# Merged additions, leaky units and stores in the three tails of a graph network

## What is computed

```python
def _sage_conv(x, src, dst, Wl, bl, Wr):
    agg = jax.ops.segment_max(x[src], dst, num_segments=x.shape[0])
    agg = jnp.where(jnp.isfinite(agg), agg, 0.0)
    return agg @ Wl + bl + x @ Wr

h = jnp.maximum(_layernorm(x, axis=-1), 0.0)
h = leaky_relu(_sage_conv(h, src, dst, Wl1, bl1, Wr1), 0.01)   # 128 -> 256
h = leaky_relu(_sage_conv(h, src, dst, Wl2, bl2, Wr2), 0.01)   # 256 -> 256
h = leaky_relu(_sage_conv(h, src, dst, Wl3, bl3, Wr3), 0.01)   # 256 -> 128
return x + h
```

## Time and profile before

| what | us |
|---|---|
| median of 3 runs | 6159.85 |
| lowest and highest of them | 6159.41, 6161.66 |
| the profiled execution, its own time | 6166.19 |
| its span | 6164.4 |
| tail of layer 0, first end-row gather to the next layer's first gather | 2004.00 to 2076.39 |
| tail of layer 1, the same | 4048.95 to 4121.35 |
| tail of layer 2, first end-row gather to the end of the span | 6094.30 to 6164.4 |

### The profile page before, as it was taken

The page is one execution under the profiler, slowest core; times in us unless marked ns, Lnnn a source line. Parts: engine busy times, 40 slices in busy tenths (PEclk is TensorE's granted clock), DMA queues, the critical chain, the costliest instruction groups (busy, mean ns, idle before and its releaser), DMA issues. The chain is left out here.

```text
span 6164.4 us, 24445 instructions
## 1 busy us (share of the span) xinstructions
PE 691.8 (11%) x2214; PEld 397.6 (6%) x2214; DVE 2907.7 (47%) x3633; ACT 227.4 (4%) x662; POOL 4617.2 (75%) x4877
## 2 busy tenths in 40 slices
PE   0111111111100770000000000056000000000003
PEld 0000000000000430000000000044000000000002
DVE  4333333333333555555555555565555555555556
ACT  1000000000000110000000000011000000000001
POOL 6777777777777777777777777767777777777776
PEclk7555555555555655555555555565555555555556
DMA  4333333333333576666666666667666666666665
GB/s 138 106 109 105 107 107 106 107 107 105 108 104 106 181 233 210 210 210 210 207 210 210 208 210 209 210 211 244 210 210 207 210 210 209 210 208 210 210 207 176
DMA packets 434293, 1088.81 MB, mean 177 GB/s; under 512 B 100293, under 2 KB 152778, under 8 KB 434266
## 3 DMA queue, kind: packets, MB, share of 16 engines
q0 software_dynamic: 206976, 530.17, 31.4%
q1 hardware_dynamic: 204506, 539.02, 23.2%
q10 hardware_dynamic: 22784, 19.34, 1.0%
HBM read 555.06 MB, written 533.07 MB: 177 GB/s over the span
## 5 line engine op out<-in xcount | busy, mean ns | idle before, releaser
L394 POOL DMA_INDIRECT ring<-features,stage x4692 | 4449.2, 948 | 1454.6 <-issue 1401.5
L715 DVE TENSOR_TENSOR ring<-banks,ring 128x1024 f32<-128x1024 f32 (+1 forms) x1173 | 1226.9, 1046 | 3057.5 <-DMA ring<-features,stage 3040.3
L687 DVE TENSOR_TENSOR banks<-ring,banks 128x1024 f32<-128x1024 f32 (+1 forms) x1173 | 1231.9, 1050 | 37.5
L940 PE MATMUL banks<-ident,ring 128*128 128x128 f32 x20 | 5.0, 428 | 3772.8 <-DVEq L727 3772.8
L914 PE MATMUL banks<-dst_low,own 128*128 128x394 bf16 x200 | 98.9, 495 | 1465.8 <-DVE own L663 1465.8
L940 PEld LDWEIGHTS banks<-ident,ring 128*128 128x128 f32 x20 | 3.9, 222 | 3774.2 <-DVEq L727 3548.7
L898 PE MATMUL banks<-wr,h_turned 128*128 128x256 f32 (+1 forms) x490 | 202.7, 556 | 96.2 <-ACT h_turned L1032 96.2
L1076 ACT ACTIVATE agg<-zeros 128x512 f32<-128x512 f32 x75 | 47.3, 630 | 3955.9 <-PE banks L971 3955.9
L421 POOL DMA_INDIRECT ring<-running_max_log,end_row x147 | 142.5, 970 | 67.4 <-issue 43.9
L668 DVE COPY stage<-edges 128x8 int32 (+1 forms) x588 | 143.1, 243 | 84.8 <-DVE banks L687 25.8
L900 PE MATMUL banks<-b,ones 1*128 1x256 f32 (+1 forms) x294 | 140.3, 573 | 0.0
(11 more groups left out here) (110 smaller groups left out, 571.1 us busy)
## 6 DMA issues: line engine op xcount, KB each, us to landing
running_max_log<-ring SPq DMA_DIRECT2D x782, 512.0 KB, 3.3
running_max_log<-ring SPq DMA_DIRECT2D x391, 256.0 KB, 2.2
ring<-features,stage POOLq DMA_INDIRECT x4692, 2.8
h_in<-features ACTq DMA_DIRECT2D x98, 128.0 KB, 2.8
features<-h_out SPq DMA_DIRECT2D x48, 256.0 KB, 2.3
h_in<-features ACTq DMA_DIRECT2D x49, 64.0 KB, 1.8
out<-h_out SPq DMA_DIRECT2D x24, 128.0 KB, 2.3
ring<-running_max_log,end_row POOLq DMA_INDIRECT x147, 2.9
```

The costliest lines, as they stand in the source:

```text
L394: pool.indirect_dma_start(ring[:, c * w:(c + 1) * w], None, tables[l], bass.IndirectOffsetOnAxis(ap=stage[:, b, u:u + 1].bitcast(U32), axi ...
L687: dve.tensor_tensor(sum_ps[:, 0:CHAINS * w].rearrange("p (h f) -> p h f", h=CHAINS), group(g - 1).rearrange("p (h f) -> p h f", h=CHAINS), ...
L715: dve.tensor_tensor(group(g), sum_ps[:, 0:CHAINS * w], group(g), ALU.max).then_inc(turn, 1)
```

## The change

From now on a tail has units: `UNITS` joins pairs 0 and 1, 2 and 3, up to 18 and 19 into ten units of two pairs, and pairs 20 to 24 stay alone (`SINGLES = 5`), 15 units in all. `add_own`, `leaky`, `residual` and the store work on a unit: an addition or leaky unit of a double unit is 2 x 2n wide, 1024, 1024 and 512 elements in the three layers. A double unit's addition stands on DVE behind the `guard` of the pair after the unit, its leaky unit one step later. The projections use four neighbouring PSUM banks (1 to 4) in turn, so that a double unit lies in two neighbouring banks; `z_sum` has two buffers of twice the size, `h_out` three of twice the size. `add_own` waits in addition until the unit two before it is done, and PE waits for the unit that held its bank. `mask`, `guard` and `turn_pair` stay pair by pair.

```diff
-STORES = 5
+STORES = 3
+SINGLES = 5
...
+    UNITS = [(q, q + 1) for q in range(0, PAIRS - SINGLES, 2)] + [(q,) for q in range(PAIRS - SINGLES, PAIRS)]
+    UNIT_OF = [u for u, pairs in enumerate(UNITS) for _ in pairs]
...
-        z_sum = [sb(f"z_sum{b}", [P, 2 * F_MAX]) for b in range(3)]
-        h_out = [sb(f"h_out{k}", [P, 2 * F_MAX]) for k in range(STORES)]
+        z_sum = [sb(f"z_sum{b}", [P, 4 * F_MAX]) for b in range(2)]
+        h_out = [sb(f"h_out{k}", [P, 4 * F_MAX]) for k in range(STORES)]
...
-        mm_ps = [banks[:, 1, :], banks[:, 2, :], banks[:, 3, :]]
+        mm_ps = banks[:, 1:5, :]
...
+                def of_unit(u):
+
+                    first, pairs, wide = UNITS[u][0], len(UNITS[u]), PAIR_TILES[UNITS[u][0]] * n
+
+                    def rows(tile, at):
+                        return tile[:, at:at + pairs * wide].rearrange("p (k f) -> p k f", k=pairs)
+
+                    b = first % 4
+                    return (mm_ps[:, b:b + pairs, 0:wide], rows(z_sum[u % 2], 0), rows(h_out[u % STORES], 0),
+                            rows(own, first * 2 * n), rows(own, (TILES * n if l == LAYERS - 1 else 0) + first * 2 * n))
+
+                def add_own(u):
+
+                    projected, z, _, own_part, _ = of_unit(u)
+                    dve.wait_ge(z_ready, PAIRS * l + UNITS[u][-1] + 1)
+                    if u >= 2:
+                        dve.wait_ge(h_done, len(UNITS) * l + u - 1)
+                    dve.tensor_tensor(z, projected, own_part, ALU.add).then_inc(sum_done, 1)
+
+                def leaky(u):
+
+                    projected, z, made, _, _ = of_unit(u)
+                    kept = PER_OUT * l + DMA * (u // STORES)
+                    dve.wait_ge(sum_done, len(UNITS) * l + u + 1)
+                    if l < LAYERS - 1:
+                        if kept:
+                            dve.wait_ge(h_stored[u % STORES], kept)
+                        dve.scalar_tensor_tensor(out=made, in0=z, scalar=SLOPE, in1=z,
                                                  op0=ALU.mult, op1=ALU.max).then_inc(h_done, 1)
...
+                def units_ending(q):
+                    return [u for u, pairs in enumerate(UNITS) if pairs[-1] == q]
...
-                    if q >= 2:
-                        leaky(q - 2)
+                    for u in units_ending(q - 2):
+                        leaky(u)
                     if q < PAIRS:
                         guard(q)
-                    if 1 <= q <= PAIRS:
-                        add_own(q - 1)
-                    if q >= 2 and l == LAYERS - 1:
-                        residual(q - 2)
+                    for u in units_ending(q - 1):
+                        add_own(u)
+                    if l == LAYERS - 1:
+                        for u in units_ending(q - 2):
+                            residual(u)
...
-                    if q >= 3:
-                        pe.wait_ge(h_done, PAIRS * l + q - 2)
+                    if q >= 4:
+                        pe.wait_ge(h_done, len(UNITS) * l + UNIT_OF[q - 4] + 1)
...
-                for q in range(PAIRS):
-                    sp.wait_ge(h_done, PAIRS * l + q + 1)
-                    tiles = PAIR_TILES[q]
-                    rows = made[q * 2 * P:(q * 2 + tiles) * P, :]
+                for u, pairs in enumerate(UNITS):
+                    sp.wait_ge(h_done, len(UNITS) * l + u + 1)
+                    tiles = sum(PAIR_TILES[q] for q in pairs)
+                    rows = made[pairs[0] * 2 * P:(pairs[0] * 2 + tiles) * P, :]
```

More of the change, by code:

```diff
@@ L69, in gnn_program @@
     SIGNED = STEPS * BLOCKS + 1
-    assert TILES % 2 == 0 and PAIRS % STORES == 0 and (BLOCKS - 1) * BLOCK_COLS < LAST
+    assert TILES % 2 == 0 and len(UNITS) % STORES == 0 and (BLOCKS - 1) * BLOCK_COLS < LAST
     assert LAST % CHAINS == 0 and KC_MAX * RUNS <= 2 * BANK and CHAINS * F_MAX <= 2 * BANK
@@ L265, in gnn_program @@
         CHUNKS_TO = [sum(k for k, _ in shapes[:l]) // P for l in range(LAYERS + 1)]
-        PER_OUT = PAIRS // STORES * DMA
+        PER_OUT = len(UNITS) // STORES * DMA
         FIRSTS = (STEPS - 1) * BLOCKS + sum(width(b, True) > CHAINS for b in range(BLOCKS))
@@ L818, in guard @@
                                         ).then_inc(agg_done, 1)
-                def add_own(q):
-                    b = q % 3
-                    dve.wait_ge(z_ready, PAIRS * l + q + 1)
-                    wide = PAIR_TILES[q] * n
-                    dve.tensor_tensor(z_sum[b][:, 0:wide], mm_ps[b][:, 0:wide],
-                                      own[:, q * 2 * n:q * 2 * n + wide], ALU.add).then_inc(sum_done, 1)
-                def leaky(q):
-                    b = q % 3
-                    kept = PER_OUT * l + DMA * (q // STORES)
-                    wide = PAIR_TILES[q] * n
-                    dve.wait_ge(sum_done, PAIRS * l + q + 1)
+                def of_unit(u):
[5 more added lines that the diff above has]
+                            rows(own, first * 2 * n), rows(own, (TILES * n if l == LAYERS - 1 else 0) + first * 2 * n))
@@ L834, in leaky @@
                     if l < LAYERS - 1:
                         if kept:
-                            dve.wait_ge(h_stored[q % STORES], kept)
-                        dve.scalar_tensor_tensor(out=h_out[q % STORES][:, 0:wide], in0=z_sum[b][:, 0:wide],
-                                                 scalar=SLOPE, in1=z_sum[b][:, 0:wide],
+                            dve.wait_ge(h_stored[u % STORES], kept)
+                        dve.scalar_tensor_tensor(out=made, in0=z, scalar=SLOPE, in1=z,
                                                  op0=ALU.mult, op1=ALU.max).then_inc(h_done, 1)
@@ L840, in leaky, with residual @@
                     else:
-                        dve.scalar_tensor_tensor(out=mm_ps[b][:, 0:wide], in0=z_sum[b][:, 0:wide],
-                                                 scalar=SLOPE, in1=z_sum[b][:, 0:wide],
+                        dve.scalar_tensor_tensor(out=projected, in0=z, scalar=SLOPE, in1=z,
                                                  op0=ALU.mult, op1=ALU.max).then_inc(leaked, 1)
-                def residual(q):
-                    b = q % 3
-                    wide = PAIR_TILES[q] * n
-                    dve.wait_ge(leaked, q + 1)
-                    dve.wait_ge(h_stored[q % STORES], PER_OUT * l + DMA * (q // STORES))
-                    dve.tensor_tensor(h_out[q % STORES][:, 0:wide], mm_ps[b][:, 0:wide],
-                                      own[:, TILES * n + q * 2 * n:TILES * n + q * 2 * n + wide],
-                                      ALU.add).then_inc(h_done, 1)
+                def residual(u):
+                    projected, _, made, _, h0_part = of_unit(u)
+                    dve.wait_ge(leaked, u + 1)
+                    dve.wait_ge(h_stored[u % STORES], PER_OUT * l + DMA * (u // STORES))
+                    dve.tensor_tensor(made, projected, h0_part, ALU.add).then_inc(h_done, 1)
@@ L897, in own_project @@
                     for c in range(kc):
-                        pe.matmul(mm_ps[p][:, 0:n], h_turned[p][:, c, :], wr_sb[l][:, c, :],
+                        pe.matmul(mm_ps[:, p, 0:n], h_turned[p][:, c, :], wr_sb[l][:, c, :],
                                   start=(c == 0), stop=False)
-                    pe.matmul(mm_ps[p][:, 0:n], ones[0:1, :], b_sb[l][:, :],
+                    pe.matmul(mm_ps[:, p, 0:n], ones[0:1, :], b_sb[l][:, :],
                               start=False, stop=True).then_inc(own_mm, 1)
@@ L1040, in keep_own @@
                     act.wait_ge(weights_loaded, N_WEIGHTS)
-                    nc.scalar.activation(own[:, bass.ds(j * (2 * n) + p * n, n)], mm_ps[p][:, 0:n],
+                    nc.scalar.activation(own[:, bass.ds(j * (2 * n) + p * n, n)], mm_ps[:, p, 0:n],
                                          ACT.Copy).then_inc(own_done, 1)
```

6 lines of the change are left out of this document (3 added, 3 removed).

## The result

With the change the median is 6173.26 us (16 runs, 6162.75 to 6175.2) against 6160.62 before (16 runs, 6159.41 to 6163.11): 12.6 us more. The ratio of the means is 1.0019 with a 95% interval of 1.0013 to 1.0026. It is slower, by about the 0.2% that can just be told from no change, and outside the range that I gave.

What follows compares the result with a forecast made beforehand. POOL's gathers bound the scans, which the change leaves alone, and pace the tails, where DVE barely keeps up. Tails 1, 0 and 2 sum 6.4 + 0 + 0.4 = +6.8 on 6159.85: 6166.6 us, range 6160.0 to 6171.0.

Steps and rivals of the forecast that it cites:

- The loop in tail 1: Layer 1's tail: wide additions wait for PE's projection, 5.70 us for two pairs against POOL's 5.13; +6.4 us for the tail.
- the gathers of tail 1 as before: Sign expected in the changed kernel's profile: POOL's end-row gathers in layer 1's tail unchanged.
- The start and end of tail 1: Layer 1's tail: first wide addition at 4061.54, guard 3 at 4064.42; mask 22 at 4116.9, its delay passing to layer 2's scan.
- Tail 0, the step that failed: Layer 0's tail: POOL, at 5.14 us for two pairs, stays slower than DVE, so 0 change.
- my own sign of being wrong: Wrong if tail 1's odd guards come every 5.1 us, or tail 0 or a scan changes by over 1 us.
- the second rival: Fewer instructions decide: DVE gains 1.2 us in tail 1, POOL's stretched gathers lose up to 1.7 in tails 0 and 1; 6157, 8%.
- 4.65 us for two pairs: Layer 0's tail: DVE's worst case with PE at its lower clock, against 5.14 from POOL.
- Stores: All tails: 15 stores instead of 25, up to 512 KB; longer bursts may delay a gather, 0 to +1 us.
- Tail 2: Layer 2's tail: no loop, but the steps of pairs 20 and 21 take 4.89 us against 4.44; +0.4 us.
- The projection was not ready in time: Judges the first rival: projection ready in time, only touching mask and guard count, 5.04 against 5.13 us; 6160.8, 15%.
- PE's clock stayed up: Judges the third rival: PE's clock falls in tail 1, total passing 12.3 us more, near 6200 if the whole tail; 8%.
- An instruction's cost in a full queue: DVE: a 1024-wide instruction costs 1.14 us in the queue, 1.229 alone; two narrow ones 1.20, so a merging saves 0.06.

Runs made afterwards that it cites:

- e3: The changed kernel with layer 1's tail in single pairs but for the first two: 6160.56 us, ratio 1.0007.
- e1: The changed kernel with the leaky unit reading the sum from PSUM and the own part from SBUF (one SBUF input, not a leaky unit's result): 6160.9 us, ratio 1.0009.
- e5c: The changed kernel with one store for each pair instead of one for each double unit: 6160.6 us, ratio 1.0010.
- e8c: The changed kernel with layer 1's tail in single pairs but for the first two, and one SBUF input in every leaky unit: 6151.62 us, ratio 0.9997.
- e4c: The kernel before the change with one SBUF input in the leaky unit (not a leaky unit's result): 6150.44 us, ratio 0.9995.

## Why the prediction was wrong, point by point

- **The loop in tail 1**: right in place, order and size. 5.67 us for 5.70, an idle time of 0.61 at each wide addition, 1.14 for a wide instruction, 0.85 for touching mask and guard (0.88). Taking it out (`e3`) gives 5.5 us back in the medians and 7.5 in the tail's length. The sign "the gathers of tail 1 as before" failed: they last 1059 ns for 977. `e1` shows that this costs nothing there, so it is luck that the term is right without it.
- **The start and end of tail 1**: 1.0 and 0.5 too low. I let PE's transposes and second projection keep the lengths that they had at the higher clock, though the clock rises in that very stretch and rose a little later. That it did is an accident of the execution; that the loop, slower than POOL, cannot make it good follows from the forecast, and I did not draw it. And a last store that lands 0.5 later had no term; with stores of one pair it does not (`e5c`, `e3`).
- **Tail 0, the step that failed.** "POOL's gathers last 0.982 there against 0.948 in the scan, 1.7 us over 49. I do not know why, and leave it." The row was the sign of a collision that the change makes longer: a gather that starts in a leaky unit of twice the width is held up for longer, 0.58 us in the mean in place of 0.16. It cost 2.84 us in place of 0, and my own sign of being wrong, a tail 0 changed by more than 1 us, came true. I had asked only whether DVE keeps POOL's pace, not what DVE does to that pace. In the second rival I had it as something that would shrink; it grew, since there are half as many leaky units but each covers twice as much, and nine gathers still started in one, where eleven had. (The 4.65 us for two pairs of that paragraph is too low besides: unlike the sum of tail 1 it leaves out the time from the guard to the projection. That did not decide, since POOL stays the slower one.)
- **Stores**: "0 to +1" is not settled. 0.5 us at the end of tail 1 is theirs. Large and small stores differ by 3.9 us in the whole (`e5c`), but 1.1 of that was there before the first store, and 2.0 go with DVE's step against POOL's. The causes do not simply add: 5.1 (`e1`) + 5.5 (`e3`) is 10.6 of 11.1, and with 3.9 for the stores more than there is.
- **Tail 2**: +0.4 forecast, 0 measured. The gather that was late in the middle of the last pairs before was late here too, within the bounds.
- **The rivals.** The projection was not ready in time. Fewer instructions brought nothing that shows. PE's clock stayed up at 80 to 84% busy (8.07 of 10 us, 16.77 of 20); the tail that got longer most got so by the loop. That the time came out above the forecast is due to a mechanism that none of the three was, though the second had it with the wrong sign.
- **The range** ended at 6171.0. Measured were 6173.3, +12.6 for +6.8. The terms that are missing are tail 0 (2.8) and tail 1's start and last store (1.2 net); tail 2 had 0.4 too much. That makes the 10.5 of the traces. Some 2 us more lie in the medians and in no trace, as the only profiled execution of the change lies 10 us under the median of the others. The median of before, 0.8 higher than the one I started from, does the rest. So tail 0 is the largest missing term, but not the whole of the miss.
- **An instruction's cost in a full queue** was read rightly: 1.13 to 1.14 us for a length of 1.22. But the section of the Trainium skill that I held against the rows ("VectorE: DVE Perf Modes", The DRAIN you can't avoid) also says that a next op that is not held starts earlier, so page and trace do not differ as flatly as I wrote.

## What to carry to other kernels

Before an operation is merged or moved on an in-order engine, count what stands between an operand's producer and its use: here two instructions fewer meant a wait at every step, and a loop through two engines set the pace, not either engine's load. Where POOL issues indirect DMAs on the critical path, a DVE instruction with two SBUF inputs beside it is not free, and making it longer makes it dearer; an operand left in PSUM avoids that. A row that is a few per cent longer in one stage than in another, for no known reason, is a term of the sum and needs bounds like any other.

## What the runs showed of the hardware that I had not expected

- A gather of POOL that is issued while DVE works on two SBUF inputs lasts its 0.95 us plus what is left of the DVE instruction, less 0.12 to 0.14 us; a DVE instruction that starts 0.05 us or more into a gather costs it nothing.
- Scans with the same code in the same set differ between executions: up to their tails they take 2002.41, 1972.07 and 1972.12 us in the profiled execution of `e8c`, 6160.92 us, where its other ten took 6150.5 to 6153.7, and 2000.45, 1968.64 and 1968.78 in that of `e4c`. That is 9 us in 5938. One profiled execution is no measure of 10 us in 6160.
- DVE and POOL can fall into step. In tail 1 of the change eight wide leaky units in a row stretch one gather each, always 0.40 to 0.42 us into the unit and by 0.67 us, so that four gathers take 4 x 1.25 + 0.67 = 5.67 us, just what DVE's loop takes. Where the two stand to each other, a collision, or its absence, repeats through many units.
